# A cross-attention and expert kernel: logits, and the second half of D of three contexts, turned by VectorE in 32 x 32 blocks; orders of all engines written anew

## What is computed

```python
def reference(x, ctx, Wq, bq, Wk, bk, Wv, bv, w_router, w_gating, w_gate, w_up, w_down):
    h = layernorm(x)                                     # (16, 112, 256)
    q, k, v = h @ Wq + bq, ctx @ Wk + bk, ctx @ Wv + bv
    x = x + softmax(q @ k.T / 16) @ v
    h = layernorm(x)
    shares = softmax(h @ w_router) * softmax(h @ w_gating / 0.1)      # over 8 experts
    shares /= shares.sum(-1) + 1e-9
    g, u = h @ w_gate[e], h @ w_up[e]                    # F = 1024, for each expert e
    return x + sum_e shares[e] * ((silu(g) * u) @ w_down[e])
```

## Time and profile before

| | us |
|---|---|
| median of 3 runs | 967.94 (967.89 to 982.71) |
| the profiled execution | 967.62 |
| its span | 965.8 |
| TensorE busy | 961.3 |
| GpSimd busy | 797.9 |
| VectorE busy | 737.3 |
| ScalarE busy | 485.3 |

### The profile page before, as it was taken

How to read it: one execution, slowest core, us unless ns; L and a number is a source line. 1 busy time by engine, 2 the same in 40 slices (tenths; PEclk the granted TensorE clock), 3 DMA queues, 4 the chain that set the end, 5 groups by cost and what they waited for, 6 DMA issues and landing times.

```text
span 965.8 us, 14829 instructions
## 1 busy us (share of the span) xinstructions
PE 961.3 (100%) x5136; PEld 892.9 (92%) x5136; DVE 737.3 (76%) x1264; ACT 485.3 (50%) x859; POOL 797.9 (83%) x640
## 2 busy tenths in 40 slices
PE   9999999999999999999999999999999999999998
PEld 7999899999999999999999999999999999999998
DVE  4987347777778777787877787778887778777995
ACT  7997554444544444544545444445445454445441
POOL 5999966767788888888988888888898888888884
PEclk9999999999999999999999999999999999999999
DMA  7441131411010111021100110011100200111135
GB/s 207 144 125 42 40 101 34 149 63 42 23 35 32 42 42 44 23 63 42 39 27 22 41 63 23 23 63 42 44 22 23 75 30 23 39 47 42 39 51 141
DMA packets 58339, 53.43 MB, mean 55 GB/s; under 512 B 17892, under 2 KB 54216, under 8 KB 58264
## 3 DMA queue, kind: packets, MB, share of 16 engines
q1 hardware_dynamic: 58256, 52.48, 17.9%
q10 hardware_dynamic: 8, 0.00, 0.0%
HBM read 45.07 MB, written 5.56 MB: 52 GB/s over the span
## 4 chain that ended last, share of the span: by engine, by line
PE 99%; DVE 0%; issue 0%; DVEq 0%
PE ps L329 96%; PE ps L1755 1%; PE ps L1864 1%; PE ps L1791 1%; PE ps L1743 0%; PE ps L1808 0%; PE ps L1834 0%; PE ps L1701 0%; PE ps L1859 0%; DVE w_raw L1430 0%; DVEq L85 0%; DVE lg L1486 0%; PE ps L1707 0%; PE ps L1987 0%; DVEq L1428 0%
## 5 line engine op out<-in xcount | busy, mean ns | idle before, releaser
L329 PE MATMUL ps<-arena 128*128 128x448 f32 (+5 forms) x2064 | 387.8, 339 | 0.0
L329 PEld LDWEIGHTS ps<-arena 128*128 128x128 f32 (+2 forms) x2064 | 343.7, 186 | 21.5 <-POOL arena L616 0.4
L622 POOL TENSOR_TENSOR arena<-shared,arena 128x448 fp32r<-128x448 f32 x196 | 252.6, 1303 | 125.3 <-ACT arena L1005 117.7
L329 PE MATMUL ps<-xc_hi,w_hi 128*128 128x448 f32 x904 | 331.1, 366 | 0.0
L329 PE MATMUL ps<-xc_hi,w_lo 128*128 128x448 f32 x904 | 330.2, 365 | 0.0
L329 PE MATMUL ps<-xc_lo,w_hi 128*128 128x448 f32 x904 | 330.2, 365 | 0.0
L329 PEld LDWEIGHTS ps<-xc_hi,w_hi 128*128 128x128 f32 x904 | 169.8, 188 | 13.8 <-DVE cw_rows L1455 0.4
L329 PEld LDWEIGHTS ps<-xc_hi,w_lo 128*128 128x128 f32 x904 | 169.8, 188 | 13.6
L329 PEld LDWEIGHTS ps<-xc_lo,w_hi 128*128 128x128 f32 x904 | 169.9, 188 | 13.1
L998 ACT ACTIVATE shared<-shared 128x448 f32<-128x448 f32 x180 | 101.6, 580 | 146.4 <-DVE shared L1365 74.6
L739 POOL TENSOR_TENSOR xsacc<-xsacc,xf 128x448 f32<-128x448 f32 x104 | 119.2, 1157 | 0.0
(11 more groups left out here) (165 smaller groups left out, 1159.9 us busy)
## 6 DMA issues: line engine op xcount, KB each, us to landing
early<-in_L_ffn_w_down SPq DMA_DIRECT2D x16, 512.0 KB, 3.8
xf<-cw_dram SPq DMA_DIRECT2D x16, 448.0 KB, 4.8
shared<-in_ctx SPq DMA_DIRECT2D x16, 336.0 KB
w_raw<-in_L_ffn_w_gate SPq DMA_DIRECT2D x17, 256.0 KB, 2.8
w_raw<-in_L_ffn_w_up SPq DMA_DIRECT2D x17, 256.0 KB, 3.2
early<-in_L_ffn_w_gate SPq DMA_DIRECT2D x15, 256.0 KB, 2.8
early<-in_L_ffn_w_up SPq DMA_DIRECT2D x15, 256.0 KB, 3.2
xsacc<-in_x SPq DMA_DIRECT2D x8, 224.0 KB, 4.8
```

The source lines that it names most:

```text
L329: ins = nc.tensor.matmul(dst, w, m, start=first and i == 0, stop=last and i == len(passes) - 1, skip_group_check=onto)
L622: nc.gpsimd.tensor_tensor(h[:, 1, j, at:at + TC], tile, h[:, 0, j, at:at + TC].bitcast(fp32), ALU.subtract).then_inc(hid_lo_done, 1)
```

## The change

**Contexts 12, 13 and 14** (pairs 6, and b = 0 of pair 7). Their rows are loaded in natural order (partition p holds rows p, 125 + p, 250 + p). `transpose_ctx` on TensorE turns only the first half of D (three matmuls). The second half is loaded a second time by `load_blocks`, four DMAs of 32 partitions each that place 32 x 32 blocks (12 blocks of rows, pieces of 128 bytes), into `u21_odd` or into free slots of `w_raw0`; VectorE's `turn_ctx` turns all blocks in one transpose of 128 x 384 into the bank of that half. `ct_high` waits for both.

**Logits.** `transpose_logits` moves from TensorE to VectorE: four transposes of 32 partitions x 224 for each half cp, and `logits_ready` counts four for each.

**Orders.** The lists of all five engines up to the quads are new.

```diff
-                for k in range(DK):
+                for k in range(1 if 2 * p + b in BY_BLOCK else DK):
                     for t in range(KT):
                         at = t * D + k * P
                         ins = nc.tensor.transpose(ps_c[:, k, t * KP:(t + 1) * KP], ctx_raw[:, p % 2, b, at:at + P], ident[0:KP, 0:KP])
...
-            def transpose_logits(cp):
-                pe.wait_ge(lt_kept, 2 * (cp + 1))
...
-                for i in range(RT):
-                    ins = nc.tensor.transpose(ps_l[:, i, :, :].rearrange("p l n -> p (l n)"), lt_f[:, i * P:(i + 1) * P], ident[0:4 * E, 0:4 * E])
-                ins.then_inc(logits_ready, 1)
...
+            def load_blocks(p, b):
+                i = BY_BLOCK[2 * p + b]
+                if i == 1:
...
+                at_least(sp, cb_turned, i - 1)
+                at = (2 * p + b) * TK
+                for j in range(P // Q):
+                    cols = slice(P + j * Q, P + (j + 1) * Q)
+                    src = ctx_rows[at:at + CB * Q, cols].rearrange("(i s) e -> s i e", s=Q)
+                    dst = blocks[i % 2][j * Q:(j + 1) * Q, :].rearrange("s (i e) -> s i e", e=Q)
+                    sp.dma_start(dst, src).then_inc(blocks_in[i % 2], DMA)
...
+            def turn_ctx(p, b):
+                i = BY_BLOCK[2 * p + b]
+                ve.wait_ge(blocks_in[i % 2], P // Q * DMA * (i // 2 + 1))
+                split_or_kept(ve, ct_hi_done, ct_lo_done, 2 * p + b - 1, 2 * FULL)
+                nc.vector.transpose(ps_cb, blocks[i % 2]).then_inc(cb_turned, 1)
...
             def ct_high(p, b):
                 sc.wait_ge(ct_ready, 2 * p + b + 1)
+                if 2 * p + b in BY_BLOCK:
+                    sc.wait_ge(cb_turned, BY_BLOCK[2 * p + b] + 1)
...
-                    sc.wait_ge(logits_ready, 1)
+                    sc.wait_ge(logits_ready, P // Q)
...
+            def transpose_logits(cp):
+                ve.wait_ge(lt_kept, 2 * (cp + 1))
+                if cp == 0:
+                    ve.wait_ge(mix_done, PAIRS)
+                else:
+                    ve.wait_ge(logits_done, cp)
+                for i in range(P // Q):
+                    src = lt_f.rearrange("n (t i q) -> n t i q", i=P // Q, q=Q)[:, :, i, :]
+                    dst = ps_l[i * Q:(i + 1) * Q, :, :, :].rearrange("p t l n -> p t (l n)")
+                    nc.vector.transpose(dst, src).then_inc(logits_ready, 1)
```

More of the change, by code:

```diff
@@ L35, in xattn_ffn_kernel @@
     HSLOTS = 4
+    Q = 32
     FULL = 2
+    BY_BLOCK = {b: i for i, b in enumerate([12, 13, 14])}
+    CB = -(-TK // Q)
     TURNED = range(CP, GROUPS - CP)
     UNITS = 4
-    Q = 32
     BACKS = (P // Q) ** 2
@@ L170, in xattn_ffn_kernel @@
         u22 = up_t[:, 2, :]
+        blocks = [u21[1][:, 0:CB * Q], w_raw0[:, 0, 4:8, :].rearrange("p s f -> p (s f)")[:, 0:CB * Q]]
         lt = up_t[0:4 * E, 0:2, :]
@@ L437, in _ @@
             keep_x1(3)
+            load_set(3)
             load_down(0)
@@ L674, in _ @@
             norm2(1)
+            low_set(1)
             cn_low(5, 0)
@@ L678, in _ @@
             norm2(2)
-            low_part(0, "first")
[L680 to L684, removed]
+            cn_low(6, 0)
+            cn_low(6, 1)
+            root2(3)
+            add_bv(6)
+            norm2(3)
+            low_part(0, "first")
             cn_low(7, 0)
+            low_part(0, "second")
             cn_low(7, 1)
-            low_part(0, "second")
             root2(4)
-            low_part(0, "s2")
             norm2(4)
@@ L1161, in _ @@
-            plain_silu(2, 2)
+            plain_high(1, 3)
+            plain_silu(2, 0)
+            keep_routed(1, 1)
+            plain_high(2, 0)
+            plain_silu(2, 1)
+            plain_high(2, 1)
+            plain_silu(2, 2)
+            shares_exp()
+            high_part(0, "s4")
             plain_silu(2, 3)
-            plain_high(2, 1)
+            plain_high(2, 2)
+            plain_high(2, 3)
             high_set(2)
@@ L1610, in _ @@
             residual1(6)
+            plain_hidden(0, 2)
             stats2(6)
-            plain_hidden(0, 2)
+            plain_hidden(0, 3)
             at_low(7)
-            plain_hidden(0, 3)
             residual1(7)
@@ L2020, in _ @@
             transpose_weights(1)
+            keep_busy(1)
             key_bias_row()
-            keep_busy(1)
+            merged_weights()
+            transpose_ctx(0, 0)
             query_bias()
-            transpose_ctx(0, 0)
-            merged_weights()
             transpose_norm(0)
@@ L2100, in _ @@
             scores(6, 0)
+            transpose_norm(7)
+            scores(6, 1)
             transpose_ctx(7, 0)
-            transpose_norm(7)
+            transpose_mix(5)
             values(4)
-            scores(6, 1)
-            transpose_mix(5)
+            transpose_probs(6, 0)
+            transpose_probs(6, 1)
+            queries(7)
             transpose_norm2(3)
+            mix_ctx(6)
             transpose_ctx(7, 1)
-            transpose_probs(6, 0)
-            queries(7)
-            transpose_probs(6, 1)
+            scores(7, 0)
@@ L2126, in _ @@
-            plain(0, 0, 2)
-            transpose_mix(7)
-            plain(0, 1, 2)
-            plain(0, 0, 3)
+            plain(0, 0, 2)
+            plain(0, 1, 2)
+            values(6)
+            mix_ctx(7)
+            plain(0, 0, 3)
+            transpose_mix(7)
+            plain(0, 1, 3)
+            route(0, 0)
             transpose_norm2(5)
-            plain(0, 1, 3)
+            plain(1, 0, 0)
             values(7)
-            plain(1, 0, 0)
-            route(0, 1)
             plain(1, 1, 0)
```

438 lines of the change are left out of this document (219 added, 219 removed).

## The result

The changed kernel takes 970.93 us, median of 20 runs (lowest 969.37), against 968.05 for the kernel before, also 20 runs (lowest 967.27): ratio 1.0029, 95% interval 1.0022 to 1.0036. It is slower by 0.3%, where 965.8 was forecast and 968.4 was the top of the range. Most kernels here, the one before too, have some executions 14 to 17 us longer, and in the four profiles of such a one (`set2_later`, `cw_down`, `cw_noctx`, `cw_between`) the surplus lies in the long last piece (793.5 instead of 778.74 us); the ratios leave them out, and so do all medians from here on, which for these two kernels are 970.47 and 967.88. The profiled execution took 971.15 us.

A forecast was written before the change was run, and what follows sets the result against it. TensorE, busy 961.3 of 965.8 us, was taken as the bound. 967.62 - 0.96 (contexts) - 1.46 (logits) + 0.3 (waits) = 965.5, and the median lying 0.32 above gave 965.8 us; range 964.8 to 968.4.

The forecast's parts named there:

- What bounds the kernel: Whole kernel: TensorE's queue sets the time; its unbroken piece of 778.74 us from 183.17 us on stays the same.
- The logits, -1.46: Two groups of seven logits transposes leave TensorE, 0.73 us each: 1.46 us saved.
- The contexts, -0.96: Batches 12 to 14: nine transposes of 0.107 us leave TensorE, 0.96 us saved; VectorE's 1.6 us of turns covered.
- VectorE's transposes, 0.53 and 0.35: Lengths on VectorE: 0.53 us for a context's 128 x 384, 0.35 us for a logits transpose of 32 x 224.
- The slack of 1 us at `plain_hidden(2, 1)`: Second four logits transposes: product ready at 4.7 us, TensorE needs it at 5.7, one microsecond left.
- The DMAs: Block loads for three batches: 0.80 us per issue, 3.2 us of SP's queue per batch, landing covered by slack.
- The third rival: Block loads from HBM in 128-byte pieces land late; 12 us landing would give 967.8 us; chance 0.05.
- I put 0.6 us of new waits against 0.3 gained: +0.3, bounds -0.4 and +2.4.: New orders: TensorE's new waits, reckoned from pair 7's last handovers, less waits filled, add 0.3 us.
- The factor of 1.74: VectorE: two SBUF operands take 1088 ns against 625 with PSUM; upper bound of 0.92 us for a context's transpose.
- Given back: Feeding engines near 90% busy up to 80 us: 1 to 2.4 us come back, middle 967.4 us; chance 0.17.
- Slower: Logits transposes before keep_logits(1) last 1.3 us each on VectorE, giving 969.6 us; decides from 0.6 us; chance 0.08.
- A granted clock below 1.00: Any stretch with a granted clock below 1.00 would show the forecast wrong; no size given.

The follow-up runs named there:

- set2_later: The changed kernel with one GpSimd call, low_set(2), moved behind plain_low(3, 1): 966.84 us, 0.9995 of the kernel before.
- cw_down: `cw_later` with TensorE's down(0, 0) moved up behind plain(3, 0, 0): 967.13 us, 0.9996 of the kernel before.
- cw_noctx: `cw_later` with all contexts turned by TensorE, without block loads and turn_ctx: 967.81 us, 1.0002 of the kernel before.
- cw_between: `best3` with VectorE's combine_weights one call earlier, behind plain_hidden(3, 0): 966.88 us, 0.9993 of the kernel before.
- old_logits: The kernel before, in its own orders, with only the logits' transposes moved to VectorE: 966.14 us, 0.9988 of the kernel before.
- old_ctx: The kernel before, in its own orders, with only the three contexts' second halves turned by VectorE: 967.85 us, 1.0003 of the kernel before.
- best3: `cw_down` with ScalarE's high_set(2) moved behind plain_silu(3, 1): 968.03 us, 1.0006 of the kernel before.
- cw_later: The changed kernel with VectorE's combine_weights moved behind plain_hidden(3, 1): 967.29 us, 0.9997 of the kernel before.
- old_both: The changed kernel's VectorE transposes, contexts and logits, with all five engines in the orders of the kernel before: 966.9 us, 0.9993 of the kernel before.
- collide: `old_logits` with combine_weights moved beside GpSimd's low_set(2), plain rows added behind plain_hidden(3, 3): two executions 969.30 and 968.23 us.
- best4: `best3` with keep_busy ahead of context (1, 0)'s transposes and VectorE's stats1(4) behind times_bk(1): 968.91 us, 1.0015 of the kernel before.

## Why the prediction was wrong, by its steps

- **What bounds the kernel, and "from 183 us on nothing changes".** Right: 778.74 us with 3906 matmuls in both.
- **The logits, -1.46.** Right to the hundredth (`old_logits`). A group goes with its edges, by starts and not by the chain's piece of 0.54.
- **The contexts, -0.96.** 0.85 in the new orders (`cw_noctx`), nothing in the old ones (`old_ctx`). The step that called 1.6 us on VectorE covered by the free 2.7 of 20 us was too easy: a share of free time says nothing of whether it is free where the turn stands, as `old_ctx` shows. In the new orders it held, with VectorE busy 19.27 of 20 us between 60 and 80 us; what in them makes the room was not tried.
- **VectorE's transposes, 0.53 and 0.35.** Measured 0.58 to 0.59 and 0.42. Short by a tenth and a fifth. In the changed kernel the contexts' turns cost TensorE nothing; four of the logits' take 1.78 us with the steps between them, where the chain had 1.4.
- **The slack of 1 us at `plain_hidden(2, 1)`.** It was used up, 0.41 us beyond: by 0.4 us of transposes, and by 0.9 of the subtraction of the maximum, 1.33 us instead of 0.39, with two SBUF operands and beside GpSimd. Where the subtraction takes 1.13 (`best3`) and 1.02 (`cw_later`), TensorE's step at this place is 0.41 and 0.31 us instead of 0.61. The chain added up VectorE's operations by their lengths in the trace of before, and there the subtraction, at 124.34, fell into a gap of 0.08 us between two of GpSimd's sums; the sum behind it took 0.96 us where its neighbours took 0.73.
- **The DMAs.** Issue 0.54 instead of 0.80 (the third group's four took 2.14 us), landing 2.4 to 3.6 us, median 2.7, from HBM in pieces of 128 bytes. The third rival falls; nothing waited.
- **"I put 0.6 us of new waits against 0.3 gained: +0.3, bounds -0.4 and +2.4." This is the step that failed.** It was a guess by the density of GpSimd's and VectorE's work, drawn from pair 7's handovers, and looked at neither of the places that decided. The order alone is worth 186.77 - 182.08 = +4.7 us from `old_both` to the changed kernel: 4.2 of waits at 123, 127 and 134 us, 1.5 of clock, 0.3 of longer steps behind the waits, less what the contexts gain in it (0.85, where they lost 0.33 in the old orders). Two readings were there to be had. `combine_weights` had moved behind `plain_hidden(2, 3)`, and `low_set(2)` runs on GpSimd at that point, 4.07 us in the trace of before. And `down(0, 0)` to `(0, 2)`, the cover of the two table loads, had moved further back. In its place the runs show 3.6 us lost ahead of 187 us where 2.1 were to be gained, the larger part by one multiplication of 0.36 us that stood for 3.98 (`cw_later` and `set2_later` win back 4.2 us of the chain).
- **The factor of 1.74** in the contexts' paragraph fits this mechanism, though no run tests it there: 1088 ns for an operation on two SBUF operands against 625 for one with PSUM, and the 60 that make the 1088 go from 615 to 1976. The prediction used it as the upper bound of a transpose, which has one operand and is not held up, and not for the operations that do have two. As a mean of 60 it also hides the price: it isn't a factor, but the rest of whatever GpSimd is doing, up to 3.8 us here.
- **Rivals.** *Given back* said 967.4 and named the crowded stretch to 80 us; that is `old_ctx` (967.85), not the changed kernel. *Slower* had the side, and its 969.6 is nearest to the 970.9 measured, but its mechanism (transposes of 0.6 us and more) fell with 0.42. *A granted clock below 1.00* stood among what would show the prediction wrong, with no price on it.

The Trainium skill, "SBUF — State Buffer", section "Who interferes with whom", says that a VectorE instruction with two inputs in SBUF contends with a GpSimd instruction that reads SBUF, that the shared port pair is an exclusive lock, and that issue order decides who blocks. The traces agree: 3.98 and 4.13 us for an operation of 0.36, both ending 0.2 us behind GpSimd's, while reduces, reciprocals and operations with a PSUM operand kept their length. The section also names `tensor_scalar` among what can contend, which the 3.87 us of `best3` bear out. The prediction did not weigh this rule. By the trace of before, an estimate: the multiplication at the start of an operation of 4.07 us ends 4.07 - 0.36 = 3.7 us late, ahead of a `plain_hidden` that TensorE needs.

## What to carry to other kernels

When an order changes, take the short operations of VectorE that have all their operands in SBUF (here those on two tensors and a TENSOR_SCALAR; reduces and reciprocals passed) and lay each beside what GpSimd runs at that moment: its price is not its length but the rest of GpSimd's operation, and it matters where something that TensorE needs is queued behind it. Then ask of each call that moved away what it had been covering (here two table loads of 1.28 us), because the call itself costs the same everywhere and its cover doesn't. Where the slack is about a microsecond, a call moved on one engine carries others with it on the next, so such an order is judged by the timelines of all engines side by side; the smallest edit, the logits alone in the old orders, was as good as the best searched order.

## What the runs showed of the hardware

- A multiplication of 128 x 112 on VectorE took 0.36 us with GpSimd idle, 0.98 beside operations of 1.16, and 3.98 and 4.13 beside one of 4.02 and 4.06: it ends 0.2 us behind GpSimd's. A TENSOR_SCALAR on 128 x 14, with one tensor operand, was held as well: 0.71 and 3.87 us instead of 0.17. Reduces, reciprocals and 32 x 32 transposes were not, in any of these runs.
- TensorE's standstill of 2.43 us was followed by nine steps at a granted clock of 0.50 (137.8 to 141.1 us), which cost 1.5 us more. Not in every execution: of 15 executions of the changed kernel five have a mean clock of 0.998 (median 971.83 us) and ten 1.000 (median 969.95), a difference of 1.9 us. A wait of 1.73 us in `collide` left the clock at 1.00. `best3` and `best4` stand alike for 1.9 us, and behind it the same 135 matmuls take, first in `best3`, then in `best4`, whose granted clock is 0.56 from 143 to 146 us:

```profile
140.88 20.64 PE ps L339 x135
```

```profile
141.20 22.12 PE ps L339 x135
```

  What decides it between two executions stays open.
- VectorE's transposes into PSUM: 0.42 us for 32 x 224 and 0.59 for 128 x 384, in fp32. Four of the small ones take 1.78 us at 119.25, all beside a sum on GpSimd, and 1.77 at 109.74, where GpSimd is idle for the first 1 us.
